# Homes of buffers: x1 and the second feed-forward weights 64 bytes out of step with their partners

## The chip, the cores and the metric

The kernel runs on one core of a Trainium2 chip, as one program. The metric is the device time of one execution in microseconds (us), the median of several runs. TensorE multiplies, VectorE (DVE), ScalarE (ACT) and GpSimd (POOL) do the elementwise work, and SyncE (SP) issues most DMAs.

## The reference

Tokens x (32 sequences of 32 tokens, width 256, so 1024 tokens) go through an adaLN-conditioned transformer layer, a feed-forward layer with ternary weights, and a residual sum, all in float32.

```python
ada = cond @ ada_w + ada_b                       # six vectors of 256 per sequence
shift1, scale1, gate1, shift2, scale2, gate2 = split(ada, 6)
x1 = ln(x) * (1 + scale1) + shift1
q, k, v = split(x1 @ qkv_w + qkv_b)              # 16 heads of 128
attn = softmax(q @ k.T * 128 ** -0.5) @ v        # within a sequence
x = x + gate1 * (attn @ out_w + out_b)
x2 = ln(x) * (1 + scale2) + shift2
h = gelu(x2 @ ffn_w1 + ffn_b1)                   # 256 -> 1024
y = x + gate2 * (h @ ffn_w2 + ffn_b2)            # 1024 -> 256
# ternary layer on y: rms norm, int8-like rounding, weights in {-1, 0, 1} times a scale
g = silu(bit(y, w1, g1)) * bit(y, w2, g2)
return x_in + bit(g, w3, g3)
```

## The kernel before, in words

Tokens lie on the 128 partitions in tiles of 128, two tiles to a quarter of 256 tokens, so there are four quarters. The 16 heads form four groups of four. A unit is one quarter with one group: 16 units, `u` from 0 to 15. The first eight run over groups 0 and 1, quarter by quarter; the last eight over groups 2 and 3, and between them the feed-forward layers of the quarters that have all their heads. The order on each engine is written out by hand, with semaphores between engines; no planner decides it.

A float32 product of full precision is made of three products in the float32r format, in `three_pass` (the matmul is at L570): each operand is split into a high part and a low part (`_hi`, `_lo`), and high times high, high times low and low times high are accumulated in PSUM. Each matmul has a stationary operand, which TensorE loads first (the profile's LDWEIGHTS, PEld), and a moving operand that streams past it (PE, MATMUL). The load for the next matmul runs beside the matmul before it. These are the users of `three_pass`:

- `qk_unit`: q and k of one head for a quarter. The weight columns (`w_hi`, `w_lo`) are stationary, x1 (`x1_hi`, `x1_lo`) moves. 128x256, three passes of two.
- `v_unit`: x1 is stationary, the weight columns move. 128x512, three passes of two.
- `out_proj`: the attention result (`at_hi`, `at_lo`) is stationary, the output weights (`wo_hi`, `wo_lo`) move. 128x256, three passes of four.
- `ffn1`: the weights `f1_hi`, `f1_lo` are stationary, x2 moves; it lies in x1's buffers of the quarter.
- `ffn2`, `late_ffn2`, `end_ffn2`: the hidden rows `h_hi`, `h_lo` (placed over `stage`) are stationary, the weights `f2_hi`, `f2_lo` move.

In the profile the names are cut: `x_hi` is x1_hi, `f_hi` f1_hi or f2_hi, by its partner. In a row the moving operand is named first and the stationary one second.

Between the products stand short matmuls: `score` (L633) and `attend` (L663) on blocks of 32 rows, transposes, and the ternary products `z_product` (L855), whose stationary rows `qt_bf` lie over `x1_lo`.

Buffers in SBUF are given out by `Floor`, one after another in the order of the `sb(...)` calls; each length is rounded up to 32 bytes. Lengths per partition: the x1, f1, f2 halves 8192 bytes each, w 12288, wo, q, k, v and at 4096, stage 16384, scores and probs 1024. row_max and row_sum have 32 bytes each and lie between scores and probs. This gives the addresses modulo 512 in the table of the section on the change. Other views (`h_hi`, `qt_bf`, `tern_odd`, `late_...`) are laid over these buffers by `at(...)` and follow them.

Of the kernel before, what the change touches and what calls it, by code (L numbers as in the profile page):

```python
# [6 lines left out]
F32R = mybir.dt.float32r  # L7
# [7 lines left out]
P = 128  # L15
# [13 lines left out]
class Count:  # L29
# [5 lines left out]
    def up(self, instruction):  # L35
        instruction.then_inc(self.sem, 1)
        self.n += 1
        return self.n


class Floor:
# [19 lines left out]
def adaln_bitffn(nc, x, cond, ada_w, ada_b, qkv_w, qkv_b, out_w, out_b, ffn_w1, ffn_b1, ffn_w2, ffn_b2,  # L61
                 w1, g1, w2, g2, w3, g3, out):
    NB, TB, D = x.shape
# [10 lines left out]
    MT = MLP // P  # L74
# [39 lines left out]
    with ExitStack() as ctx:  # L114
        floor = Floor(nc)
        sb, at = floor.new, floor.at
# [14 lines left out]
        xin = sb("xin", [P, NT, D])  # L131
        x1_hi = sb("x1_hi", [P, NQ, KD, QT], F32R)
        x1_lo = sb("x1_lo", [P, NQ, KD, QT], F32R)
        CH = 2 * KD * HW
        VW = KD * GC
        SLOT = HALVES * CH
        WO = SLOT + VW
# [4 lines left out]
        stage = sb("stage", [P, WO + HG * D])  # L142
        f1_hi = sb("f1_hi", [P, KD, MLP], F32R)
        f1_lo = sb("f1_lo", [P, KD, MLP], F32R)
        f2_hi = sb("f2_hi", [P, MT, D], F32R)
        f2_lo = sb("f2_lo", [P, MT, D], F32R)
        q_t = sb("q_t", [P, HG, QT])
        k_t = sb("k_t", [P, HG, QT])
        v_sb = sb("v_sb", [P, 2, GC])
# [268 lines left out]
        def _(sp):  # L418
            def load_qk(g, c):
                for s in range(2):  # L420
                    c0 = s * INNER + g * GC + c * HW
                    sp.dma_start(stage[:, c * CH + s * KD * HW:c * CH + (s + 1) * KD * HW].rearrange(
                        "p (k c) -> p k c", k=KD), qkvw_d[:, :, c0:c0 + HW]).then_inc(qkw_in[c], 16)
# [134 lines left out]
        def _(pe):  # L558
# [14 lines left out]
            def qk_unit(u, h, late=None):  # L573
# [11 lines left out]
                for s in range(2):  # L585
                    cols = [slice(c * CH + (s * KD + k) * HW + r * P, c * CH + (s * KD + k) * HW + (r + 1) * P)
                            for k in range(KD)]
# [528 lines left out]
        def _(dve):  # L1116
# [64 lines left out]
            def low_qk(c):  # L1181
                s = slice(c * CH, (c + 1) * CH)
                dve.wait_ge(qk_hi, c + 1)
                dve.tensor_tensor(w_lo[0][:, s], stage[:, s], w_hi[0][:, s].bitcast(F32), ALU.subtract).then_inc(qk_lo, 1)
# [18 lines left out]
            def split_qk(g, c):  # L1203
                s = slice(c * CH, (c + 1) * CH)
                dve.wait_ge(qkw_in[c], 32 * (g + 1))
                if g >= 2:
                    dve.wait_ge(projected, NPROJ * (g + 4) + 2 * (c + 1))
                dve.tensor_copy(w_hi[g % 2][:, s], stage[:, s]).then_inc(qk_hi, 1)  # L1208
# [529 lines left out]
        def _(act):  # L1738
# [32 lines left out]
            def high_qk(g, c):  # L1771
                s = slice(c * CH, (c + 1) * CH)
                act.wait_ge(qkw_in[c], 32 * (g + 1))
                act.copy(w_hi[g][:, s], stage[:, s]).then_inc(qk_hi, 1)
# [511 lines left out]
```

## Time and profile before

| | us |
|---|---|
| median of 3 runs | 326.51 (326.22 to 327.21) |
| the profiled execution | 326.65 |
| its span, first to last instruction | 324.5 |
| TensorE busy | 314.2 (97%) |
| weight loads busy | 281.3 (87%) |
| VectorE busy | 224.2 (69%) |
| ScalarE busy | 183.6 (57%) |
| GpSimd busy | 125.4 (39%) |

The page gives busy time as the union of the records of an engine. Matmuls are pipelined: a record begins when the matmul starts and ends when its last result is out, so records of neighbours overlap, and the distance between starts is what a matmul takes of the engine. A timeline row merges equal neighbours; the distance between the starts of two rows, over the number of matmuls between, is the mean distance.

### The profile page before, as it was taken

Reading aid. Unit: us, or ns where it says so; the run is one execution under the profiler, and the core shown is the slowest. Engines: PE = TensorE matmul, PEld = TensorE weight load, DVE = VectorE, ACT = ScalarE, POOL = GpSimd, SP = SyncE. Lnnn points to the kernel's source line nnn. Section 1 sums busy time; section 2 is a strip of 40 time slices with the busy share of each in tenths; the row PEclk is TensorE's granted clock in tenths of the full one; section 3 lists DMA queues with packets and bytes.
Section 4 is the critical chain, followed back from the end, with each engine's and each line's share of the span. In section 5 each row is a group of like instructions: output and inputs, shape, how many; then the busy total and the mean of one; then the engine's idle time right before and its main releaser. Section 6 shows DMA issues by size and latency. Waiting matters only on the chain.

```text
span 324.5 us, 9866 instructions
## 1 busy us (share of the span) xinstructions
PE 314.2 (97%) x4197; PEld 281.3 (87%) x4197; DVE 224.2 (69%) x448; ACT 183.6 (57%) x356; POOL 125.4 (39%) x111
## 2 busy tenths in 40 slices
PE   8999999999999999999999999999999999997986
PEld 8979989899998989988998998879998889996665
DVE  3837885954995984515567148789177688887996
ACT  2646384555435574457434826587354866477694
POOL 2347405000940882665320612247330264115491
PEclk9999999999999999999999999999999999999999
DMA  7991990500048442110020000200110200200011
GB/s 239 299 347 56 291 319 4 150 16 2 2 110 217 127 140 96 56 45 2 3 68 4 0 26 11 66 2 2 34 34 2 65 4 2 67 0 2 0 34 65
DMA packets 21026, 24.41 MB, mean 75 GB/s; under 512 B 1972, under 2 KB 18520, under 8 KB 20984
## 3 DMA queue, kind: packets, MB, share of 16 engines
q1 hardware_dynamic: 20608, 23.50, 24.3%
q8 instruction: 33, 0.54, 0.7%
q10 hardware_dynamic: 376, 0.30, 0.3%
q14 instruction: 9, 0.07, 0.1%
HBM read 22.68 MB, written 1.11 MB: 73 GB/s over the span
## 4 chain that ended last, share of the span: by engine, by line
PE 83%; ACT 6%; DVE 4%; issue 2%; DMA 2%; SPq 1%; POOL 0%; DVEq 0%; ACTq 0%
PE proj_banks L570 39%; PE out_bank L570 16%; PE wide_banks L570 5%; PE turn_bank L570 4%; PE att_banks L663 3%; PE proj_banks L633 3%; PE wide_banks L855 2%; DMA stage<-in_L_cond_qkv_w 2%; PE att_banks L570 2%; ACT at_hi L1761 1%; PE wide_banks L663 1%; ACT work L1886 1%; PE att_banks L855 1%; DVE v_sb L1253 1%; PE wide_banks L738 1%
## 5 line engine op out<-in xcount | busy, mean ns | idle before, releaser
L1752 ACT ACTIVATE q_t<-proj_banks,bias_cols 128x256 f32<-128x256 f32 x64 | 30.4, 475 | 50.7 <-PE proj_banks L570 50.2
L570 PE MATMUL proj_banks<-x_hi,w_hi 128*128 128x256 f32 x252 | 54.0, 296 | 0.3 <-ACT k_t L1752 0.2
L570 PE MATMUL proj_banks<-x_lo,w_hi 128*128 128x256 f32 x252 | 50.7, 283 | 0.0
L570 PE MATMUL proj_banks<-x_hi,w_lo 128*128 128x256 f32 x252 | 50.6, 282 | 0.0
L570 PEld LDWEIGHTS proj_banks<-x_hi,w_hi 128*128 128x128 f32 x252 | 39.4, 191 | 4.1 <-issue 2.0
L570 PEld LDWEIGHTS proj_banks<-x_hi,w_lo 128*128 128x128 f32 x252 | 39.2, 191 | 0.0
L570 PEld LDWEIGHTS proj_banks<-x_lo,w_hi 128*128 128x128 f32 x252 | 39.2, 191 | 0.0
L1253 DVE TENSOR_TENSOR v_sb<-proj_banks,bv_row 128x512 f32<-128x512 f32 x32 | 21.7, 684 | 23.9 <-PE proj_banks L570 14.5
L1752 ACT ACTIVATE k_t<-proj_banks,bias_cols 128x256 f32<-128x256 f32 x64 | 30.0, 469 | 0.0
L570 PE MATMUL out_bank<-wo_hi,at_hi 128*128 128x256 f32 x128 | 21.5, 290 | 0.6
L2096 POOL TENSOR_TENSOR w_lo<-stage,w_hi 128x1024 fp32r<-128x1024 f32 x6 | 14.3, 2396 | 19.9 <-DVE w_hi L1208 14.3
L570 PE MATMUL proj_banks<-w_hi,x_hi 128*128 128x512 f32 x64 | 20.7, 405 | 0.4 <-ACT k_t L1752 0.4
L2155 POOL TENSOR_TENSOR h_lo<-work,h_hi 128x512 fp32r<-128x512 f32 x10 | 12.9, 1292 | 18.8 <-ACT h_hi L1839 18.3
L570 PE MATMUL out_bank<-wo_lo,at_hi 128*128 128x256 f32 x128 | 19.9, 278 | 0.0
L570 PE MATMUL proj_banks<-w_lo,x_hi 128*128 128x512 f32 x64 | 19.9, 391 | 0.0
L570 PE MATMUL out_bank<-wo_hi,at_lo 128*128 128x256 f32 x128 | 19.9, 277 | 0.0
L570 PE MATMUL proj_banks<-w_hi,x_lo 128*128 128x512 f32 x64 | 19.8, 391 | 0.0
L2127 POOL TENSOR_TENSOR xa<-xa,out_b_row 128x512 f32<-128x512 f32 x4 | 5.2, 1294 | 35.1 <-ACT xa L1768 35.1
L570 PEld LDWEIGHTS out_bank<-wo_hi,at_hi 128*128 128x128 f32 x128 | 17.3, 188 | 1.5 <-issue 0.9
L1279 DVE STREAM_TRANSPOSE att_banks<-att_banks 128x512 f32<-128x512 f32 x16 | 11.6, 724 | 9.7 <-PE wide_banks L663 8.4
L570 PEld LDWEIGHTS out_bank<-wo_lo,at_hi 128*128 128x128 f32 x128 | 17.1, 188 | 0.0
L570 PEld LDWEIGHTS out_bank<-wo_hi,at_lo 128*128 128x128 f32 x128 | 17.0, 188 | 0.0
(327 smaller groups left out, 786.2 us busy)
## 6 DMA issues: line engine op xcount, KB each, us to landing
stage<-in_L_cond_qkv_w SPq DMA_DIRECT2D x16, 256.0 KB, 4.6
gate<-gate_rows_scratch SPq DMA_DIRECT2D x48, 64.0 KB, 2.4
stage<-in_L_cond_qkv_w SPq DMA_DIRECT2D x4, 512.0 KB, 6.0
stage<-in_L_cond_out_w SPq DMA_DIRECT2D x16, 128.0 KB, 3.6
work<-in_L_ffn_w SPq DMA_DIRECT2D x2, 1024.0 KB, 9.8
xin<-in_x SPq DMA_DIRECT2D x7, 256.0 KB, 2.9
bv_row<-in_L_cond_qkv_b SPq DMA_DIRECT2D x4, 256.0 KB, 5.5
work<-in_L_cond_ada_w SPq DMA_DIRECT2D x1, 1024.0 KB, 9.9
```

The source lines that it names most:

```text
L570: mm = pe.matmul(dst, l, r, start=start and i == 0, stop=stop and i == len(seq) - 1)
L633: mm = pe.matmul(packed[j * TB:(j + 1) * TB, cols], q_t[:, h, tok], k_t[:, h, tok], start=True, stop=True)
L663: mm = pe.matmul(dst, probs_t[r, t * HG + h, :], v_sb[r, t, h * P:(h + 1) * P], start=True, stop=True)
L738: mm = pe.transpose(dst[:, m * P:(m + 1) * P], tern[p % 2][:, c0:c0 + P], ident_h[:, :])
L855: mm = pe.matmul(banks[i][:, :], qt_bf[:, b, t, i * KD + k, :], w12t[:, i, k, c * MC:(c + 1) * MC], start=(k == 0), stop=(k == KD - 1))
L1253: dve.tensor_tensor(v_sb[:, t, :], proj_bank[t][:, :], bv_row[:, u % 2, :], ALU.add).then_inc(v_kept, 1)
L1279: dve.transpose(att_from(u, p), attended_rows(u, p)).then_inc(at_turned, 1)
L1752: act.activation(dst[:, h, :], proj_bank[h % 2][:, s * QT:(s + 1) * QT], ACT.Identity, bias=bias_cols[:, c:c + 1]).then_inc(qk_kept, 1)
L1761: act.copy(att_to(at_hi, p), att_from(u, p)).then_inc(at_hi_made, 1)
L2096: pool.tensor_tensor(w_lo[g % 2][:, s], stage[:, s], w_hi[g % 2][:, s].bitcast(F32), ALU.subtract).then_inc(qk_lo, 1)
L2127: pool.tensor_tensor(xa[:, :, :], xa[:, :, :], rows, ALU.add).then_inc(acc_biased, 1)
L2155: pool.tensor_tensor(h_lo[:, m, :], hf(2 * j, 2), h_hi[:, m, :].bitcast(F32), ALU.subtract).then_inc(h_lo_made, 1)
```

## The change

Two lines move and one is added. `f2_hi` and `f2_lo` are given out right behind `x1_lo` instead of behind `f1_lo`, and then 64 bytes are left free. All that comes after, the attention weights first, moves up by 64 bytes modulo 512 (the buffers between x1 and q move by 16384 more). The end of the used space is 64 bytes higher. No operation, wait, semaphore or order changes.

| buffers | address modulo 512 before | after |
|---|---|---|
| x1_hi, x1_lo (qt_bf over x1_lo) | 480 | 480 |
| f2_hi, f2_lo | 480 | 480 |
| w_hi, w_lo, wo_hi, wo_lo | 480 | 32 |
| stage (h_hi, h_lo), f1_hi, f1_lo | 480 | 32 |
| q_t, k_t, v_sb, scores | 480 | 32 |
| probs_t, at_hi, at_lo, xa, xt, gates | 32 | 96 |
| w12t, w3t | 32 | 96 |

```diff
@@ -36,6 +36,9 @@
+STEP = 64
@@ -131,6 +134,9 @@
         xin = sb("xin", [P, NT, D])
         x1_hi = sb("x1_hi", [P, NQ, KD, QT], F32R)
         x1_lo = sb("x1_lo", [P, NQ, KD, QT], F32R)
+        f2_hi = sb("f2_hi", [P, MT, D], F32R)
+        f2_lo = sb("f2_lo", [P, MT, D], F32R)
+        floor.next += STEP
         CH = 2 * KD * HW
@@ -142,8 +148,6 @@
         stage = sb("stage", [P, WO + HG * D])
         f1_hi = sb("f1_hi", [P, KD, MLP], F32R)
         f1_lo = sb("f1_lo", [P, KD, MLP], F32R)
-        f2_hi = sb("f2_hi", [P, MT, D], F32R)
-        f2_lo = sb("f2_lo", [P, MT, D], F32R)
         q_t = sb("q_t", [P, HG, QT])
```

## Rows read from the trace of the kernel before

**Rows 1.** The page: busy TensorE and granted clock in 40 equal slices (tenths).
```profile
PE   8999999999999999999999999999999999997986
PEclk9999999999999999999999999999999999999999
```
**Rows 2.** The page: shares of the chain that ended last, by engine, by line.
```profile
PE 83%; ACT 6%; DVE 4%; issue 2%; DMA 2%; SPq 1%; POOL 0%; DVEq 0%; ACTq 0%
PE proj_banks L570 39%; PE out_bank L570 16%; PE wide_banks L570 5%; PE turn_bank L570 4%; PE att_banks L663 3%; PE proj_banks L633 3%; PE wide_banks L855 2%; DMA stage<-in_L_cond_qkv_w 2%; PE att_banks L570 2%; ACT at_hi L1761 1%; PE wide_banks L663 1%; ACT work L1886 1%; PE att_banks L855 1%; DVE v_sb L1253 1%; PE wide_banks L738 1%
```
**Rows 3.** TensorE's groups by form: xcount | busy us, mean ns | idle before.
```profile
L570 PE MATMUL proj_banks<-x_hi,w_lo 128*128 128x256 f32 x252 | 50.6, 282 | 0.0
...
L570 PE MATMUL out_bank<-wo_lo,at_hi 128*128 128x256 f32 x128 | 19.9, 278 | 0.0
L570 PE MATMUL proj_banks<-w_lo,x_hi 128*128 128x512 f32 x64 | 19.9, 391 | 0.0
L570 PE MATMUL out_bank<-wo_hi,at_lo 128*128 128x256 f32 x128 | 19.9, 277 | 0.0
L570 PE MATMUL proj_banks<-w_hi,x_lo 128*128 128x512 f32 x64 | 19.8, 391 | 0.0
...
L855 PE MATMUL wide_banks<-w12t,qt_bf 128*128 128x512 fp8e4 x40 | 10.4, 382 | 0.0
...
L570 PE MATMUL wide_banks<-x_hi,f_lo 128*128 128x256 f32 x48 | 9.6, 282 | 0.0
...
L570 PE MATMUL turn_bank<-f_lo,h_hi 128*128 128x256 f32 x32 | 4.5, 283 | 0.0
...
L570 PE MATMUL att_banks<-x_hi,f_lo 128*128 128x256 f32 x16 | 3.2, 283 | 0.0
...
L570 PE MATMUL proj_banks<-f_lo,h_hi 128*128 128x256 f32 x16 | 3.2, 283 | 0.0
L570 PE MATMUL out_bank<-f_lo,h_hi 128*128 128x256 f32 x16 | 3.2, 282 | 0.0
```
**Rows 4.** TensorE's timeline, 34 to 40 us: start us, us, instruction, xcount.
```profile
35.70 0.62 PE L570 MATMUL out_bank<-wo_hi,at_hi 128*128 128x256 f32 x4
...
37.06 0.40 PE L570 MATMUL proj_banks<-x_hi,w_hi 128*128 128x256 f32 x2
...
39.94 0.27 PE L713 MATMUL turn_bank<-ident,gate 128*128 128x128 f32 x1
```
**Rows 5.** The same, 174.8 to 185 us.
```profile
179.20 0.63 PE L570 MATMUL out_bank<-wo_hi,at_hi 128*128 128x256 f32 x4
...
180.62 0.40 PE L570 MATMUL wide_banks<-x_hi,f_hi 128*128 128x256 f32 x2
```
**Rows 6.** The same, 283.9 to 296 us.
```profile
289.78 0.40 PE L570 MATMUL out_bank<-f_hi,h_hi 128*128 128x256 f32 x2
...
291.22 0.40 PE L841 MATMUL turn_bank<-ident_h,late_xg 128*128 128x128 f16 x4
```
**Rows 7.** Weight loads by form, columns as in rows 3.
```profile
L570 PEld LDWEIGHTS proj_banks<-x_hi,w_lo 128*128 128x128 f32 x252 | 39.2, 191 | 0.0
...
L570 PEld LDWEIGHTS out_bank<-wo_lo,at_hi 128*128 128x128 f32 x128 | 17.1, 188 | 0.0
...
L570 PEld LDWEIGHTS out_bank<-f_lo,h_hi 128*128 128x128 f32 x16 | 2.5, 191 | 0.0
```
**Rows 8.** The chain in order of time: start us, us, what.
```profile
163.64 0.70 DVE xa L1306
...
167.99 0.66 PE turn_bank L748 x4
...
209.78 0.69 ACT work L1866
...
213.16 1.63 PE proj_banks L570 x6
```
**Rows 9.** TensorE's timeline, 163 to 169 us.
```profile
163.38 0.40 PE L570 MATMUL proj_banks<-x_hi,w_hi 128*128 128x256 f32 x2
...
167.46 0.40 PE L570 MATMUL proj_banks<-x_hi,w_lo 128*128 128x256 f32 x2
```

## The prediction, made before the changed kernel ran

> **What bounds the kernel now.** I read four views, in this order. The page first: TensorE is busy 97% of the span, and in 36 of the 40 slices it is at nine tenths or more [rows 1]. VectorE, at 69%, and ScalarE, at 57%, are not the bound on average. The granted clock was 1.00 in every slice [rows 1], the upper level of 2.4 GHz, so the clock explains nothing here. Second, the chain that ended last: 83% of it is TensorE, and three quarters of that belong to one line, L570, the helper for the three-pass products [rows 2]. So a few nanoseconds on each of its matmuls are worth microseconds.
>
> Third, the matmuls grouped by form, for the distance from one start to the next. "Busy" there is the union of overlapping records, so k equal matmuls in a row fill (k-1) distances plus one duration. The projection matmuls of q and k (128x256) come in twos of one form: 50.6 us over 126 pairs is 402 ns, less the duration of 282 ns leaves 119.6 ns. The output projection has the same shape and comes in fours: 19.9 us over 32 fours is 622 ns, less 278, a third of it: 114.6 ns; its other low pass gives 115.0 [rows 3]. So the same instruction on the same engine takes 4.8 ns less in one place.
>
> What differs? Homes in SBUF. In the kernel before, x1, w, f1, f2, h (in stage), q and k all lie at the same place modulo 512 bytes, because every buffer between them is a multiple of 512 long. row_max and row_sum, 32 bytes each, come after them, so at_hi and at_lo lie 64 bytes further on than wo. The output projection is thus the one three-pass product whose stationary operand already lies 64 bytes ahead of the moving one.
>
> Fourth, the timeline, which puts the two side by side. From 35.70 to 37.06 us run twelve output-projection matmuls, 113.3 ns each; from 37.06 to 39.94, without a break, 24 q/k matmuls at 120.0 ns [rows 4]. A second level of the output projection stands at 179.20: twelve in 1.42 us, 118.3 ns [rows 5]. Is it the PSUM bank? No: the second feed-forward product into the same out_bank, with operands in step, takes twelve in 1.44 us, 120.0 ns [rows 6]. The weight loads agree: 191 ns in q/k and in the feed-forward product into out_bank, 188 ns in the output projection [rows 7].
>
> **The change part by part.** No instruction is added, removed or moved, on any engine or queue, and no wait changes; buffers get other addresses. Modulo 512, x1 and f2 stay at 480; w, wo, stage (h), f1, q, k and v go from 480 to 32; at, probs, xt, w12t and w3t from 32 to 96.
>
> *Products that come out of step with the stationary operand 64 bytes ahead*, as in the output projection: q/k (w over x1), first feed-forward (f1 over x1), second (h over f2). The counts are three forms of each row: 3x252 = 756, 3x48 + 3x16 = 192, and 3x(32+16+16) = 192, together 1140 [rows 3]. Three stretches hide some of them. From 163.64 to 167.99 the chain runs over VectorE and GpSimd [rows 8] while TensorE does 36 q/k matmuls, the first at 163.38, the last pair at 167.46 [rows 9]. From 209.78 to 213.16 it runs over ScalarE, beside some 24 matmuls, and once more one quarter later [rows 8]. That leaves 1140 - 36 - 24 - 24 = 1056, I take 1050. Price each: the fast end is 120.0 - 113.3 = 6.7 ns (7.0 us in all), the slow end 120.0 - 118.3 = 1.7 ns (1.8 us). I take the difference of the means, 119.6 - 114.8 = 4.8 ns, since it comes from 256 matmuls that stand between the same neighbours: 5.0 us.
>
> *v products* (192 of 128x512): now x1 is stationary and w moves, so the stationary operand comes to lie 64 bytes behind. No row shows that sign. Their distance now: 19.9 us over 32 pairs less 391 ns is 231, and by the other low pass 228 [rows 3]. Good end: the ternary products of the same width, fours in 10 groups, (1040-382)/3 = 219 ns, a gain of 10 ns or 1.9 us. Bad end: the effect with its sign turned, +4.8 ns, 0.9 us lost. The nearest row is their own: 0.
>
> *Output projection, scores, attention*: at over wo, q with k, and v with probs keep their distances: 0. The ternary products have qt_bf in x1_lo and w12t moving; their distance goes from 64 to 128 bytes. At 219 ns they show no sign of a conflict; 52 of them at 4.8 ns bound it to 0.25 us either way, taken as 0.
>
> *VectorE, ScalarE, GpSimd and DMA* use moved buffers too. No row shows them depending on an address. Chain shares of 6% for ScalarE and 4% for VectorE [rows 2] are 32 us; 2% of it either way would be 0.6 us. Taken as 0.
>
> *What is late next.* Where TensorE gets to a wait earlier, the wait lasts longer: the residual and normalisation of each quarter [rows 8], and the waits for v_sb and at_hi ahead of the output projections. These depend on results that come earlier too, so most of the gain passes through them; what sticks is the part of a stretch in which TensorE ran beside the waited-for chain. About 100 of the 1050 matmuls stand in such places, 0.5 us.
>
> Sum: -5.0 + 0 + 0.5 = -4.5 us. The profiled execution took 326.65 us (span 324.5), 0.14 above the median of the runs; from 326.65 that makes 322.1, against the median 326.51 it makes 322.0 us.
>
> A rule speaks against all this. The Trainium skill, "TensorE: Matmul & The Clock Gate", section "Step-by-step: what each phase is for", says that TensorE has two independent read ports and that loading the next weights takes no read bandwidth from the running matmul; "SBUF — State Buffer", section "Who interferes with whom", says that PE never waits on anyone. By that the sum would be 0 and the time 326.5. The trace disagrees so far: 113.3 against 120.0 ns at one clock [rows 4], and the same bank cleared of suspicion [rows 6].
>
> **The rivals.**
> 1. *Fast lock everywhere.* The output projection settles at 113.3 ns once it has run some matmuls [rows 4]; q/k runs are as long (24 in a row there) and now follow on one another without an in-step product between. Then 1050 x 6.5 = 6.8 us, and with half of v's good end 0.9 more, less 0.7 stuck: -7.0, 319.5 us. Against it: the level of 118.3, which the trace shows to last over whole runs [rows 5].
> 2. *Slow lock.* The products settle at 118.3, as the output projection does where it follows an in-step product directly [rows 5]. 1050 x 1.7 = 1.8 us, 0.2 stuck: 324.9 us. Against it: means nearer to 113.3 (114.6 and 115.0 are a mixture of about 70% and 30%).
> 3. *The change does nothing.* Something other than the 64 bytes makes the output projection quick, its fours on one weight column pattern for instance, and q/k stays at 120: 326.5 us. For it: the rule above, and that only one product in the trace shows the effect.
> 4. *Out of step is worse for these operands.* The conflict depends on when a weight load starts inside the running matmul; in q/k pairs, with weights in rows of 256 columns, the shifted load could meet the moving stream again and settle at 124 rather than 120 ns. Then 1050 x 4 = 4.2 us more, 330.7. It decides from the point where the distance passes 120.0. For it: nothing but that lock levels exist at all; against it: both levels that the 64-byte product shows lie below 120.
>
> **How the numbers follow.** Forecast, mixture as in the output projection: 0.60, 322.0 us, its own range 320.5 to 323.5. Rival 1: 0.17. Rival 2: 0.12. Rival 3: 0.07. Rival 4: 0.04. The range from 318.9 to 324.9 takes in the forecast with the v bounds, nearly all of rival 1 and half of rival 2, and leaves some 0.15 out. A difference of 0.3%, about 1 us, is what a measurement of this kernel tells from none: faster below 325.5, which the forecast and rivals 1 and 2 are (0.88, allowing for the slow edge of rival 2), same 0.08, slower 0.04.
>
> **What would show it.** In the profile after: the forms of L570 on w, f1 and f2 with mean durations near 278 rather than 283 and weight loads of 188 rather than 191 ns; in the timeline 24 q/k matmuls in 2.72 to 2.84 us instead of 2.88; the output projection unchanged at 113 to 118; v at 226 to 231. Matmuls at 120 with a faster run, or at 114 with an unchanged one, would refute the argument: the first means that the gain came from another engine, the second that something else sets the end.

## The result, and the profile after

The changed kernel took 325.51 us (median of 20 runs, 323.37 to 327.08) against 327.12 us for the kernel before (median of 20, run beside it): a ratio of 0.9949 [0.9929, 0.9969], faster by 0.5%, or 1.6 us. Predicted were 4.5 us. The profiled run took 326.43 us (span 324.3). The granted clock, averaged over a run, splits the 20 runs in two: ten with 0.999 or 1.000 have a median of 324.75 us, ten with 0.995 one of 326.25.

The page first: busy time, TensorE's two slice rows, the chain's shares.

```profile
PE 311.4 (96%) x4197; PEld 277.9 (86%) x4197; DVE 225.5 (70%) x448; ACT 183.2 (56%) x356; POOL 125.4 (39%) x111
...
PE   8999999999999999999999999999999999997986
...
PEclk9999999999999999999999999999999999997999
...
PE 79%; DVE 8%; ACT 5%; issue 4%; DMA 2%; SPq 1%; POOL 0%; DVEq 0%; ACTq 0%
```

Against [rows 1, 2]: TensorE's busy time went down by 2.8 us (from 314.2), yet the span by 0.2, so the rest came back as idle time. VectorE's share of the last chain doubled in this run, from 4% to 8% (5% in run e9 below). Its instructions are the same, yet it was busy 1.3 us longer (225.5 against 224.2); the next part finds most of it. And one slice of the clock row, the 37th, is no longer full.

TensorE's groups and weight loads by form, columns as in rows 3:

```profile
L574 PE MATMUL proj_banks<-x_hi,w_lo 128*128 128x256 f32 x252 | 49.6, 279 | 0.0
...
L574 PE MATMUL out_bank<-wo_lo,at_hi 128*128 128x256 f32 x128 | 19.9, 278 | 0.0
L574 PE MATMUL proj_banks<-w_lo,x_hi 128*128 128x512 f32 x64 | 19.9, 393 | 0.0
```
```profile
L574 PEld LDWEIGHTS proj_banks<-x_hi,w_lo 128*128 128x128 f32 x252 | 38.3, 188 | 0.0
...
L574 PEld LDWEIGHTS out_bank<-wo_lo,at_hi 128*128 128x128 f32 x128 | 17.1, 188 | 0.0
```

This is what the prediction asked to see: q/k at 279 ns instead of 282 with loads of 188 instead of 191, output projection and v where they were [rows 3, 7]. By the prediction's own arithmetic q/k now stands at (49.6/126 x 1000 - 279) = 115 ns. The timeline of the stretch of [rows 4], columns as there:

```profile
35.77 0.62 PE L574 MATMUL out_bank<-wo_hi,at_hi 128*128 128x256 f32 x4
...
37.13 0.40 PE L574 MATMUL proj_banks<-x_hi,w_hi 128*128 128x256 f32 x2
...
39.96 0.60 PE L717 MATMUL turn_bank<-ident,gate 128*128 128x128 f32 x4
...
40.87 0.39 PE L574 MATMUL proj_banks<-x_hi,w_lo 128*128 128x256 f32 x2
41.10 0.39 PE L574 MATMUL proj_banks<-x_hi,w_hi 128*128 128x256 f32 x2
```

Twelve output-projection matmuls take 1.36 us as before, 113.3 ns each; the 24 of q/k take 2.83 us, 117.9 ns each, where they took 2.88. A microsecond later pairs follow at 0.23 us (40.87, 41.10), so q/k has both levels, as the output projection does.

### Where the gain went

Both kernels have 4197 TensorE records in the same order, so the distance from each start to the next can be compared one by one, and the differences add up to the difference of the spans. I did that for a later run of the changed kernel without the clock loss (experiment e9, span 321.8 against 324.5). The row for neighbours holds the distances below 150 ns within one product.

| distances | count | change, us |
|---|---|---|
| q/k, neighbours | 690 | -2.61 |
| first feed-forward, neighbours | 179 | -0.89 |
| second feed-forward, neighbours | 178 | -0.71 |
| output projection, neighbours | 349 | +0.25 |
| v, all, waits behind it among them | 192 | +0.84 |
| everything else | | +0.42 |
| span | | -2.70 |

So the products that were shifted gave 4.21 us (1047 distances at 4.0 ns), and 1.5 us of it came back. The largest single piece, 0.51 us, is a wait behind a v product, ahead of a transposition of `work`. VectorE rounds `work` for it in two instructions; GpSimd multiplies `gate` by `b_row` into another part of the buffer as soon as a transfer of `gate` has landed. First the changed kernel (run e9); rows of VectorE, GpSimd and TensorE, others left out, in brackets the idle time and what ended it:

```profile
193.95 1.67 DVE L1380 TENSOR_SCALAR work<-work,qscale 128x256 f32<-128x256 f32 x2
...
194.13 1.33 POOL L2148 TENSOR_TENSOR work<-gate,b_row 128x512 f32<-128x512 f32 x1 [1.22 <-DMA gate<-gate_rows_scratch]
...
195.67 0.40 PE L845 MATMUL turn_bank<-ident_h,work 128*128 128x128 f16 x4 [0.34 <-DVE work L1380]
```

the same place in the kernel before, and VectorE and GpSimd there in e7, which has the speed-up too:

```profile
196.15 0.62 DVE L1376 TENSOR_SCALAR work<-work,qscale 128x256 f32<-128x256 f32 x2
...
196.51 1.44 POOL L2144 TENSOR_TENSOR work<-gate,b_row 128x512 f32<-128x512 f32 x1 [1.39 <-DMA gate<-gate_rows_scratch]
...
197.59 0.40 PE L841 MATMUL turn_bank<-ident_h,work 128*128 128x128 f16 x4
```
```profile
193.80 0.62 DVE L1380 TENSOR_SCALAR work<-work,qscale 128x256 f32<-128x256 f32 x2
...
194.42 1.32 POOL L2148 TENSOR_TENSOR work<-gate,b_row 128x512 f32<-128x512 f32 x1 [1.65 <-DMA gate<-gate_rows_scratch]
```

Before, the rounding was done 0.8 us ahead of the transposition. In e9 TensorE did not simply come too early: the rounding itself took 1.05 us longer. Its second instruction took 1.40 us instead of 0.35, and it ended 0.15 us after GpSimd's. All 14 traces agree: where the second rounding began 0.09 us or more ahead of GpSimd's instruction (before, e1, e2, e4, e5, e7, e8, e12) it took 0.35 us; where it began between 0.02 us ahead and 0.12 us behind (after, e3, e6, e9, e10, e11) it took 1.40 to 1.49. Why the one holds the other up, no trace shows. Together with 0.13 us at a wait 4 us later, which grows in the same six traces only, this collision cost 0.64 us in e9. It is set by when a transfer lands, it came in e6 without any speed-up, and it did not come in e5, e7 and e8, which have one. The rest of the 1.5 us is 0.25 in the output projection's own distances, 0.21 at the wait for h_odd below, and 0.4 in many places, of both signs.

The second loss is one the prediction did not think of. Windows of the profiled run of the changed kernel: stretch, length, busy us of each engine with its instructions, granted clock, DMA.

```profile
290.00:294.00 4.00, 3.12 (x23) 1.88 (x21) 3.68 (x9) 3.97 (x7) 2.09 (x2) 1.00 0.00 0
294.00:298.00 4.00, 2.87 (x19) 2.90 (x20) 2.69 (x5) 2.13 (x4) 2.28 (x3) 0.70 0.01 4
298.00:302.00 4.00, 4.00 (x26) 3.00 (x25) 1.69 (x3) 0.89 (x2) 0.74 (x1) 0.88 0.00 0
```

Its timeline there, with the second feed-forward product that follows a wait for VectorE's rounding of h_odd:

```profile
295.13 0.63 PE L886 MATMUL turn_bank<-ident_h,h_odd 128*128 128x128 f16 x8 [2.01 <-issue]
295.55 0.75 PE L574 MATMUL out_bank<-f_hi,h_hi 128*128 128x256 f32 x2
296.10 0.63 PE L574 MATMUL out_bank<-f_lo,h_hi 128*128 128x256 f32 x2
296.52 0.63 PE L574 MATMUL out_bank<-f_hi,h_lo 128*128 128x256 f32 x2
```

The same place in run e9, and then in the kernel before:

```profile
294.26 0.61 PE L886 MATMUL turn_bank<-ident_h,h_odd 128*128 128x128 f16 x8 [1.99 <-issue]
294.68 0.48 PE L574 MATMUL out_bank<-f_hi,h_hi 128*128 128x256 f32 x2
295.00 0.39 PE L574 MATMUL out_bank<-f_lo,h_hi 128*128 128x256 f32 x2
295.23 0.39 PE L574 MATMUL out_bank<-f_hi,h_lo 128*128 128x256 f32 x2
```
```profile
296.84 0.61 PE L882 MATMUL turn_bank<-ident_h,h_odd 128*128 128x128 f16 x8 [1.77 <-issue]
297.25 0.48 PE L570 MATMUL out_bank<-f_hi,h_hi 128*128 128x256 f32 x2
```

In the first, pairs from 296.10 on stand 0.42 to 0.43 us apart, 213 ns a matmul, and the granted clock of the two stretches is 0.70 and 0.88: for some 3.4 us from 295.6 on TensorE ran at its lower level, 1.2 GHz. In the second, pairs stand 0.23 us apart. The second feed-forward product alone (178 distances) gained 0.71 us in e9 and lost 0.88 us in the profiled run, so the dip cost 1.6 us; the two medians above differ by 1.5. Before the change TensorE waited 1.77 us there and kept its clock; with the change it waits 2.0 us, and in part of the runs it loses it.

### The profile page after: what moved, and what is told of

Same layout as the page of the kernel before. It is cut to its first block, busy times and chain, and to the rows that moved or that the text cites. A ratio compares the mean times of both kernels' runs of the same rounds, so it can differ in the third digit from the quotient of the medians.

```text
span 324.3 us, 9866 instructions
## 1 busy us (share of the span) xinstructions
PE 311.4 (96%) x4197; PEld 277.9 (86%) x4197; DVE 225.5 (70%) x448; ACT 183.2 (56%) x356; POOL 125.4 (39%) x111
## 3 DMA queue, kind: packets, MB, share of 16 engines
HBM read 22.68 MB, written 1.11 MB: 73 GB/s over the span
## 4 chain that ended last, share of the span: by engine, by line
PE 79%; DVE 8%; ACT 5%; issue 4%; DMA 2%; SPq 1%; POOL 0%; DVEq 0%; ACTq 0%
PE proj_banks L574 35%; PE out_bank L574 16%; PE wide_banks L574 5%; PE turn_bank L574 4%; PE proj_banks L637 3%; PE att_banks L667 3%; PE wide_banks L859 2%; DMA stage<-in_L_cond_qkv_w 2%; PE att_banks L574 2%; PE wide_banks L667 1%; ACT work L1890 1%; DVE w_hi L1212 1%; PE att_banks L859 1%; ACT L1749 1%; PE att_banks L893 1%
## 5 line engine op out<-in xcount | busy, mean ns | idle before, releaser
L574 PE MATMUL proj_banks<-x_hi,w_hi 128*128 128x256 f32 x252 | 53.2, 292 | 1.4 <-ACT k_t L1756 0.8
L574 PE MATMUL proj_banks<-x_lo,w_hi 128*128 128x256 f32 x252 | 49.7, 279 | 0.0
L574 PE MATMUL proj_banks<-x_hi,w_lo 128*128 128x256 f32 x252 | 49.6, 279 | 0.0
L574 PEld LDWEIGHTS proj_banks<-x_hi,w_hi 128*128 128x128 f32 x252 | 38.7, 189 | 5.2 <-issue 3.3
L574 PEld LDWEIGHTS proj_banks<-x_lo,w_hi 128*128 128x128 f32 x252 | 38.4, 189 | 0.0
L574 PEld LDWEIGHTS proj_banks<-x_hi,w_lo 128*128 128x128 f32 x252 | 38.3, 188 | 0.0
L667 PE MATMUL att_banks<-v_sb,probs_t 32*32 32x128 f32 x512 | 16.5, 278 | 0.8 <-issue 0.8
L1761 ACT ACTIVATE scores<-scores 128x256 f32<-128x256 f32 x16 | 6.7, 416 | 18.6 <-DVE scores L1266 18.6
```

Of the source, the lines that this page charges most:

```text
L574: mm = pe.matmul(dst, l, r, start=start and i == 0, stop=stop and i == len(seq) - 1)
L667: mm = pe.matmul(dst, probs_t[r, t * HG + h, :], v_sb[r, t, h * P:(h + 1) * P], start=True, stop=True)
L1761: act.activation(scores[:, :, :], scores[:, :, :], ACT.Exp, scale=SM_SCALE).then_inc(exp_done, 1)
```

## The experiments

Every time stands beside runs of the kernel before on the same chip. The distances quoted are means over neighbours, as in the table above.

### e1: the new order of the buffers, without the 64 bytes

```diff
-STEP = 64
+STEP = 0
```

> The second feed-forward weights are given out early as in the changed kernel, but no bytes are left free behind them: all three-pass products but the output projection are in step again, as before. Theory (the 64 bytes do it): the q/k matmuls start 119.6 ns apart, v 228 to 231, the time is that of the kernel before, ratio 1.000 +- 0.002. Rival (the new order of the buffers does it, not the distance): q/k near 116 ns apart and a ratio near 0.995.

327.06 us against 326.87, ratio 1.0006 [0.9989, 1.0023]; q/k 119.7 ns.

```profile
L574 PE MATMUL proj_banks<-x_hi,w_lo 128*128 128x256 f32 x252 | 50.6, 282 | 0.0
```

The group is that of [rows 3] to the digit. The order of the homes does nothing; the 64 bytes do it.

### e2 and e12: steps of 128 and of 32

```diff
-STEP = 64
+STEP = 128      # e2;  32 in e12
```

> 128 bytes are left free instead of 64. Theory of a conflict that only needs the two streams apart: q/k, ffn1 and ffn2 at 113 to 118 ns as with 64, with the 118 ns level rarer if it is what is left of the conflict at a distance of one line; time within 1 us of the changed kernel, ratio 0.990 to 0.996. Rival, a conflict that comes back with a period of 128 bytes: 120 ns and a ratio of 1.000. The v products (the other sign, -128) should move away from 229 ns if their sign matters.

> 32 bytes left free instead of 64. If the gain falls off with the distance on either side of 64 (128 gave 118.6 ns for q/k, 64 gives 115.8): q/k at 116 to 119 ns, ratio 0.994 to 0.998. If 64 is the least distance that parts the streams: q/k at 119.7, ratio 1.000.

128: 326.61 us, 0.9983 [0.9967, 0.9999], q/k 118.6 ns, v 232.1: neither the theory (113 to 118 ns) nor the rival (120 ns) of e2 came. 32: 325.49 us against 327.0, 0.9952 [0.9935, 0.997], q/k 118.3 ns, and no run below a clock of 0.999. Both lie between in step (119.7) and 64 bytes (115.8), so it is the amount and not merely being out of step. No run has 256 bytes, so it isn't shown that 512 is the period at which the operands fall in step again. At 32 the longest wait ahead of h_odd is 1.8 us, as before the change. That makes 32 bytes worth as much as 64 in the median: a smaller gain, none of it lost to the clock.

### e5: the same distance with its sign turned

x1 and f2 are moved 64 bytes ahead of w, f1 and h, so that the stationary operand lies behind; at is given out earlier so that the output projection keeps its distance.

```diff
-        x1_hi = sb("x1_hi", [P, NQ, KD, QT], F32R)
-        x1_lo = sb("x1_lo", [P, NQ, KD, QT], F32R)
...
         f1_lo = sb("f1_lo", [P, KD, MLP], F32R)
+        floor.next += 64
+        x1_hi = sb("x1_hi", [P, NQ, KD, QT], F32R)
+        x1_lo = sb("x1_lo", [P, NQ, KD, QT], F32R)
```

> x1 and the second feed-forward weights are given out behind all weights and the 64 bytes free, so that now the weights w and f1 that are loaded (and h for the second product) lie 64 bytes behind the moving operand, and x1 64 bytes ahead of w in the v products; the output projection, scores and attention keep their distances. Theory (only the sign that the output projection has gives 113 ns): q/k, ffn1, ffn2 stay near 119 to 120, v goes to 226 or less, time near the kernel before, ratio 0.997 to 1.001. Rival (any 64 bytes part the two streams): q/k at 113 to 118 ns, ratio about 0.994.

324.71 us against 326.83, 0.9928 [0.9909, 0.9948]; q/k 115.8 ns, the feed-forward products 117.0 and 117.5, v 233.3 (230.0 before). All six runs had a clock of 1.000; the wait ahead of h_odd was 1.8 us.

```profile
L571 PE MATMUL proj_banks<-x_hi,w_lo 128*128 128x256 f32 x252 | 49.5, 278 | 0.0
```

The theory that only a stationary operand ahead helps has fallen: q/k gains as much with it behind. v pays 3 ns here and nothing in the change.

### e6: the output projection put in step

In the kernel before, at_hi and at_lo are given out ahead of row_max and row_sum, so that they lie in step with wo. Nothing else changes its distance.

```diff
         scores = sb("scores", [P, 2 * HG, TB])
+        at_hi = sb("at_hi", [P, 2, HG, P], F32R)
+        at_lo = sb("at_lo", [P, 2, HG, P], F32R)
         row_max = sb("row_max", [P, 2 * HG])
```

> The kernel before, with at_hi and at_lo given out ahead of the two 32-byte buffers instead of behind them, so that the output projection's operands come into step with wo; nothing else changes its distance. Theory (the distance alone sets the spacing): the output projection goes from about 115 to 119.6 ns apart, 384 matmuls, PE busy +1.8 us, time +1 to +1.8 us, ratio 1.003 to 1.006. Rival (the output projection is quick for another reason): 115 ns as before, ratio 1.000.

328.53 us against 326.83, 1.0048 [1.0032, 1.0064]: slower by 1.7 us. Its groups, matmul and load:

```profile
L570 PE MATMUL out_bank<-wo_lo,at_hi 128*128 128x256 f32 x128 | 20.5, 283 | 0.0
```
```profile
L570 PEld LDWEIGHTS out_bank<-wo_lo,at_hi 128*128 128x128 f32 x128 | 17.6, 191 | 0.0
```

The distance went from 115.3 to 119.7 ns and the load from 188 to 191 ns, the values of q/k in step: one product, the same code, and only the address moved. The cause, the distance of the two addresses, is shown from both sides. That the two reads get in each other's way is how I read it; no trace shows the reads themselves. The Trainium skill ("TensorE: Matmul & The Clock Gate", section "Step-by-step: what each phase is for") has the next weights loaded at no cost in read bandwidth to the running matmul; the measurement differs from it by 4.4 ns a matmul here, and the measurement decides. And 384 matmuls x 4.4 ns = 1.7 us is what the median lost (1.0 to 2.1 by the interval), so none of it need be hidden. The profiled run is 2.0 us longer than the one before: 1.5 in these products, 0.5 in the collision of VectorE and GpSimd, 0.4 in the opening, less 0.4 elsewhere.

### e7: x1 out of step alone

The 64 bytes stand behind x1_lo, and f2 stays behind f1, in step with h.

```diff
         x1_lo = sb("x1_lo", [P, NQ, KD, QT], F32R)
+        floor.next += STEP
```

> Only x1 is put out of step: the 64 bytes follow x1, and the second feed-forward weights stay behind f1, in step with the hidden rows over stage. Theory: q/k and ffn1 at 113 to 118, ffn2 (192 matmuls) at 119.6 again, 0.7 us more of PE time than in the changed kernel; ratio to before 0.995 to 0.998 when the clock is at full rate. Rival (the ffn2 part at the end of the program carries the gain, since least is hidden there): ratio 0.999 to 1.000.

324.84 us against 326.83, 0.9941 [0.9923, 0.9959]; q/k 116.0 and first feed-forward 115.9 ns, second feed-forward 119.4 and so left at the old level. One run of six, the profiled one, had a clock of 0.994. Its windows:

```profile
290.00:294.00 4.00, 2.15 (x14) 0.93 (x13) 3.82 (x7) 2.98 (x5) 2.54 (x2) 1.00 0.00 0
294.00:298.00 4.00, 3.98 (x29) 4.00 (x30) 1.57 (x4) 2.13 (x3) 2.53 (x2) 0.69 0.00 0
```

The wait ahead of h_odd is 1.9 us in it. The clock falls at the same place, with the second feed-forward product in step. So the dip does not come from that product's own speed. The time is better than the theory's 0.995 to 0.998, and it can't be told from that of the whole change (0.9949, 0.9936 in e9): what the shift of f2 adds in TensorE's distances doesn't show in the time.

### e3, e4 and e10: matmuls in the wait that precedes the dip

Eight small matmuls (two records each in the profile) into the bank that is written next go into the wait for h_odd, in the changed kernel (e3, and e10 once more on another chip) and in the kernel before (e4).

```diff
             pe.wait_ge(q_kept, 2 * a + 1)
+            keep_running(8, turn_bank)
             hq_turn(a - 1, 1, h_tiles[1])
```

> The changed kernel, with eight small matmuls of the identity (some 1.8 us) put in the wait of about 2.0 us ahead of the transposes of the hidden rows at 295 us of the profile after. Theory (half of the runs lose 1.5 us because the clock is granted at half rate for some 3 us after that wait): the clock is 1.00 in every run, all runs lie near 324.7 us, the median drops by about 0.8 us against the changed kernel, ratio to before 0.992. Rival (the dip comes by chance or from another stretch): 0.995 in about half of the runs as in the changed kernel, median 325.5, ratio 0.995; or the fillers delay the transposes and the time rises.

> The same eight small matmuls in the kernel before, whose wait there is 1.8 us and whose profile shows a clock of 1.00. Theory: nothing to win there in most runs, ratio 1.000 +- 0.002. Rival (the fillers help by themselves, or the kernel before loses clock too in part of its runs): ratio below 0.998.

> The changed kernel with the eight fillers, beside it. Theory: no run with a dip near 295 us, so its median lies below that of the changed kernel by 1.5 us times the share of dipped runs there, and equals the median of the undipped ones within 0.4 us. Rival: the same share of 0.995 here.

e3: 324.36 us, 0.993 [0.9907, 0.9953]. e10: 324.29 us against 327.0, 0.9912 [0.9896, 0.9929]. In both, 11 of 12 runs had a clock of 0.999 or more, where all were expected to; e10's other run (0.995, 328.04 us) wasn't profiled. e4: 326.83 us, 0.9996 [0.9982, 1.0011]: where the clock doesn't fall, the fillers are worth nothing. In e10 the wait is down to 0.18 us and the pairs behind it, at 295.04 and 295.28, stand 0.24 us apart:

```profile
292.16 1.95 PE L903 MATMUL turn_bank<-ident 128*128 128x128 f32 x16
294.29 0.62 PE L886 MATMUL turn_bank<-ident_h,h_odd 128*128 128x128 f16 x8 [0.18 <-DVE h_odd L1517]
```

h_odd is ready no sooner, so what the fillers save is the clock alone. The profiled run of e3 (327.69 us) is its one run at 0.995, and shows another dip, in the opening:

```profile
12.00:14.00 2.00, 0.42 (x4) 0.22 (x2) 0.30 (x1) 1.21 (x2) 0.03 (x1) 1.00 1.12 185
14.00:16.00 2.00, 1.28 (x11) 1.31 (x12) 1.73 (x5) 1.30 (x4) 2.00 (x1) 1.00 1.06 279
16.00:18.00 2.00, 2.00 (x12) 2.00 (x11) 1.11 (x3) 0.84 (x2) 1.05 (x2) 0.52 1.02 350
18.00:20.00 2.00, 2.00 (x10) 1.82 (x9) 0.00 (x0) 0.84 (x2) 0.00 (x0) 0.63 1.09 325
```

The last of the first weights landed at 12.77 us there instead of 11.04, TensorE stood still for most of 12 to 14 us, and afterwards ran at 0.52 and 0.63 of its clock. So that dip follows a late transfer; the landing varies from run to run (10.2 to 12.8 us in the 14 traces). e3's run lost 3.4 us against the median of the others and e10's 3.8, both more than the 1.5 of the dip near 295 us; whether e10's was of the same kind, no trace shows.

### e8 and e11: the fillers, and one wait at 109 us taken away

In the changed kernel TensorE waits 0.56 us at 109.0 us for the scores, because VectorE rounds w_hi (2.51 us, beside an instruction of GpSimd) ahead of the row maximum. Here `split_qk(2, 1)` goes behind the shift by the maximum; the fillers of e3 stay.

```diff
-                elif u == 6:
-                    split_qk(2, 1)
...
                 if u > 0:
                     softmax_shift(u)
+                if u == 6:
+                    split_qk(2, 1)
```

> The changed kernel with the eight fillers of the third run, and VectorE's split of the third group's second half of q/k weights (2.5 us there) moved behind the softmax shift of unit 6. Theory (what TensorE saved is taken by waits; this one took 0.5 us at 108 us of the profile after): TensorE's wait of 0.56 us there goes, the time is about 0.5 us under the changed kernel with fillers, ratio 0.990 to 0.992. Rival (the split is now late for the next step, or the wait moves on to the next one): no gain, ratio 0.993, or a new wait on q/k weights.

> Fillers and the softmax shift ahead of the split. Theory (the 0.56 us wait at 108 us was on the path): 0.3 to 0.6 us under the kernel with fillers alone. Rival (it comes back as a longer wait before unit 7's attention): within 0.2 us of it.

e8: 324.43 us against 326.83, 0.9922 [0.99, 0.9944]. e11: 323.82 us against 327.0, 0.9911 [0.9884, 0.9937], beside 0.9912 [0.9896, 0.9929] for e10 on that chip. The wait is gone from the trace in both, but the time can't be told from that with the fillers alone. e11 has the lowest median of all kernels run, 3.2 us below the kernel before. The traces tell why the wait of 0.56 us was worth so little: it is one of three that take from each other, behind the matmuls that start at 104.9, 109.3 and 113.9 us in the kernel before. The distances behind these three sum to 1.17 us before, 1.26 to 1.36 in the change with and without fillers (after, e9, e3, e10), and 1.06 and 1.11 in e8 and e11, and 1.06 and 1.07 in e1 and e4, which have no speed-up; in e8 the distance behind the third, ahead of the attention, is the longest of all traces, 0.82 us, so the rival was right there in part. By these sums the moved step is worth some 0.2 us (an estimate), less than these runs can tell.

### e9: the change once more

> The changed kernel unchanged, beside the next two on one chip. Theory (a dip of the clock near 295 us in part of the runs): some of the runs at a mean clock of 0.995 and 1.5 us above the rest, the others near 0.993 of before. Rival (the dips belonged to the chip of the first comparison): none here, and the same time as with fillers.

325.36 us against 327.0, 0.9936 [0.9899, 0.9974]; nine runs, four with a clock of 0.999 or more (323.59 to 324.49), five with 0.99 to 0.995 (325.36 to 328.94). Three of the five lie 1.3 to 2.2 us above the median of the four, two 4.3 and 4.9, so these two lost more than the one dip. The dip belongs to the changed kernel and not to the chip: of the 32 runs of the kernel before beside it one was below 0.999.

## Why the prediction was wrong

The direction was right, and so was the mechanism on TensorE; the size was not: 1.6 us came where 4.5 were forecast, and 325.5 lies above the range. 0.6 us of the distance from 322.0 is the base, since the kernel before took 327.12 us here and 326.51 in the three runs that the forecast started from. By its own steps:

**Products out of step: right in kind, 0.8 us too large.** The count agrees by luck: the prediction left 90 of 1140 out as hidden, the table counts 1047 because the last of each run has no neighbour of its own product. The price was 4.8 ns and measured 4.0. Part of that was rounding: read from all neighbours in the trace, the kernel before has 119.7 ns for q/k and 115.3 for the output projection, 4.4 apart. The rest is the mixture: neighbours at the level of 113 to 115 ns and at that of 116 to 118 are 0.47 and 0.45 of q/k, but 0.63 and 0.28 of the output projection before. So 4.2 us, not 5.0. Rivals 1 and 2 each hold for a part of the products. Rival 2's total, 1.6 us, is the one measured, but by chance: it has 1.8 us from the products and 0.2 back, where the trace has 4.2 and 1.5 and the clock besides.

**v, output projection, ternary products at nothing: right.** v stayed at 230 ns; the +0.84 us of the table is 0.64 us of longer waits behind two v products (0.51 the collision, 0.13 ahead of scores at 61 us) and 0.2 us in all the others. The output projection's 0.25 us is its own mixture, which differs from run to run (114.9 to 115.9 ns where it was out of step).

**What is late next, and VectorE and GpSimd at nothing: the step that failed.** It stood at 0.5 us, on the ground that the awaited results come earlier too, and the other engines were taken as 0 because no row showed them depending on an address. In e9, with a full clock, 1.5 us came back. At most 0.6 of it is what the prediction had in mind, waits that last longer because TensorE is there earlier (0.21 ahead of h_odd). The largest piece, 0.64 us, is the collision: what VectorE owed TensorE did not come earlier too but 1 us later than it otherwise would, because VectorE's rounding and an instruction of GpSimd, whose start a transfer sets, came to begin together. No address is needed for that, only that the engines shift against each other; with the addresses of the change it came in five of six traces (not in e8). Without the opening and the dip, 0.8 to 1.8 us come back in the traces of the change and of its versions in e8, e10 and e11. The opening itself ends 0.6 us earlier to 1.7 us later than before in the 14 traces, also where TensorE has no speed-up (0.2 and 0.4 us later in e1 and e6), so its waits tell nothing of the change.

**The clock: missing from the prediction.** It read a granted clock of 1.00 in every slice [rows 1] and concluded that the clock explains nothing. It did not ask what a longer wait would do to it. Ahead of h_odd the wait grew from 1.8 to 2.0 us, and in half of the runs the clock was below 0.999; in the profiled one it fell right behind this wait. It cost 1.5 us each: some 0.75 us in a median that lies between the two groups. That the wait is the cause is shown by e3 and e10 against the unfilled kernel (22 of 24 runs with a full clock, against 14 of 29 for the change), and by e4, where there was nothing to save.

The pieces together: -5.0 forecast for the products, 0.8 less in price, 1.5 us back, makes -2.7, the profiled run of e9; the ten full-clock runs of the first measurement give 324.75 - 327.12 = -2.4. Another 0.75 for the dip makes -1.7 to -2.0, beside -1.6 measured.

**Rival 3 and the rule behind it** have fallen by e1 and e6; rival 4 by the distances. Three readings of the prediction were loose, without weight in the sum: the five shares of L570 in [rows 2] make 66 of 83, four fifths and not three quarters; [rows 1] shows a clock of nine tenths or more in each slice, not 1.00; and the trace has 64 ternary products of 512 columns, not 52, which takes their bound from 0.25 to 0.31 us. What stays open: why 64 bytes do better than 32 or 128, and what sets which of the two levels a stretch takes; and why the clock falls in only some of the runs with the same wait (2.01 us with, 1.99 us without).

## What to carry to other kernels

Where TensorE bounds a kernel, compare the distance between starts of equal matmuls in different products; where one product is quicker, compare the addresses of its stationary and moving operands before looking at its code. A speed-up of the bounding engine shifts the engines against each other: price it against each result that comes just in time, and look for instructions of two engines that begin close together, since one may take several times as long beside the other (0.35 and 1.40 us here). Of 4.2 us, 1.5 went that way in e9. Before blaming a wait on a change, look at the same place in a run without the change: the opening's waits differ by more than the change is worth. And ask of every long wait of TensorE whether the change makes it longer: 0.2 us more cost 1.5 us of clock here in half of the runs, and some filler matmuls in the wait were cheap.

## What the runs showed of the hardware that was not expected

| distance of stationary from moving operand, bytes modulo 512 | q/k, 128x256, ns | from |
|---|---|---|
| 0 | 119.7 | before, e1 |
| 32 | 118.3 | e12 |
| 64 | 115.8 | after, e9 116.0 |
| 128 | 118.6 | e2 |
| 448 (64 behind) | 115.8 | e5 |

The wide v products (128x512), with the roles of the operands turned, react little and the other way: 230.0 ns in step, 230.3 and 230.7 in the change (after, e9), 232.8, 232.1 and 233.3 in e12, e2 and e5.

The clock and the wait for h_odd, which is read from the profiled run of each kernel; the last column counts the runs whose mean clock is on record:

| wait for h_odd in the profiled run | kernels | granted clock behind it | runs with a mean clock below 0.999 |
|---|---|---|---|
| 0.2 us (filled) | e3, e8, e10, e11 | 1.00 | 3 of 42; e3's dip was in the opening |
| 1.8 us | before, e1, e2, e5, e6, e12 | 1.00 | 1 of 126 |
| 1.9 us | e7 | fell to 0.69 in the next stretch | 1 of 6 |
| 2.0 us | after, e9 | fell to 0.70 (after), stayed at 1.00 (e9) | 15 of 29 |
